# One kernel, two edges: where code transposes by DMA end, and what stands ahead of the tail columns on TensorE

## The chip, the core and the metric

One core of a Trainium2 chip runs the whole kernel. The metric is the time of the program in microseconds (us) on the device; one execution was also profiled.

## What is computed

The input is 8 sequences of 1,024 rows of 256 (64 tiles of 128 rows). A linear attention block with a layer norm is followed by a feed-forward block whose operands are quantised to FP4 in blocks of 16, and another layer norm:

```python
q = elu(x @ Wq + bq) + 1; k = elu(x @ Wk + bk) + 1; v = x @ Wv + bv     # 16 heads of 16
k = k / sqrt(sum(k * k, -1) + 1e-6)
out = (q @ (k^T @ v)) @ Wo + bo                                          # per head, no softmax
a = layernorm(x + out) * gamma + beta;  x1 = layernorm(x + a)

def fp4_linear(x, w):      # both sides: per block of 16 scale = max|.| / 6, values on the grid 0, 0.5, 1, 1.5, 2, 3, 4, 6
    return fp4_quant_dequant(x) @ fp4_quant_dequant(w).T
h = silu(fp4_linear(x1, w_gate)) * fp4_linear(x1, w_up)                  # 704 columns
result = layernorm(x1 + fp4_linear(h, w_down))
```

## The kernel before

**Stages.** While the keys, values and queries are projected (pairs of tiles p = 0 to 31), steps t of the second part already begin beside them: from p = 24 on the loop runs first(p) and step(p - 33). After that come steps 3 to 69 alone. Step t holds the pieces of many tiles at once: gate and up products of tile t, down product of tile t - 4, attention output of tile t + 9, layer norms of tiles t + 7, t + 5 and t - 6, quantisation of a "joint" tile that holds the 256 columns of x of tile n and the 704 columns of h of tile n - 4. There are five streams written out by hand, one for each engine, each in a fixed order; semaphores with counts connect them, and an engine that waits holds up all that stands behind in its stream.

**TensorE (PE), step(t), lines 641 to 657.** gate_up(t,0) and gate_up(t,1) are 512 columns each; gate_up(t,2) takes the remaining 192 columns of gate and up (the "tails"). turn(n) (L616) transposes the dequantised tile n in eight matmuls into PSUM. scales_turn(n) (L623) transposes the scales of a tile whose codes are transposed by DMA. attend(u) is L586, down(u) ends at L639. All products are split into high and low parts, L469 to L471.

**Two ways to turn a tile.** Odd tiles are dequantised on GpSimd (POOL; L1295, L1297) and turned on PE. Even tiles n from 12 to 66 are turned by DMA before they are dequantised: turn_codes (L428) transposes the 16-bit codes into wo_sb, the scales are transposed on PE, copied by ScalarE (ACT, L788), written to DRAM (L435, two of L439) and read back spread over all partitions (L445), and POOL multiplies the two (dequantise_turned, L1286). ACT makes the high parts of a turned tile (high_x L797, high_h L811 and L814) and, for tiles turned by DMA, copies it into PSUM (L801, L819); VectorE (DVE) makes the low parts, low_x (L1069) and low_h (L1076). For even tiles the waits of PE are on these.

**Quantisation of a tile.** DVE takes block maxima (amax_x L1031, amax_h L1037) and makes scales (L1050 to L1054); POOL divides (over_scales L1264 for h, L1267 for x); ACT converts (to_f16 L773, L775) and adds a rounding constant (add_half L782); DVE cuts the low bits (cut L1062). Then comes dequantise or turn_codes.

**ACT, step(t), lines 851 to 872:** high_h(t), silu(t,0) (L827), the three layer norm applications (L834, L839, L848), silu(t,1) (L829), high_x(t+1), scales_copy(t+3), to_f16(t+3), add_half(t+3). In the merged stretch first_keys(p) follows step: k_exps (L720), k_squares (L725). **DVE, step(t), lines 1106 to 1151:** residual (L1093), cut(t+2), amax_x, ln1_sum (L1099), statistics (L1121, L1124), low_h(t), gated(t,0) (L1085), statistics (L1131), three aggregates (L1104), gated(t,1) (L1087), amax_h(t+4), low_x(t+1), joint_scales(t+4). In the merged stretch first_keys(p) then makes the key features (L946) and values (L952); the queries' features are L936. **POOL:** roots(t) makes variance plus epsilon (L1249), the negative means (L1250), the power (L1252) and the product of the two (L1255); step(t) then dequantises, divides by scales, and applies gamma and beta (L1273, L1277). **SyncE (SP)** issues the DMAs in one queue: turn_codes(t+2), loads and stores of rows, repeat_scales(t+3), which waits on its own two or three small writes before L445.

**SHIFT.** For t below 6, turn(t+1), high_x(t+1) and low_x(t+1) stand before the tails, silu(t,1) and gated(t,1), and POOL dequantises tile t + 2 in step t; from t = 6 on they stand behind, and POOL dequantises tile t + 1.

Of the kernel before, what the change touches and what calls it, by code (L numbers as in the profile page):

```python
# [10 lines left out]
ALU = mybir.AluOpType  # L11
# [16 lines left out]
def after(eng, sem, count):  # L28

    if count > 0:  # L30
        eng.wait_ge(sem, count)


def build(nc, x, Wq, bq, Wk, bk, Wv, bv, Wo, bo, gamma, beta, w_gate, w_up, w_down, out):
# [24 lines left out]
    with ExitStack() as ctx:  # L59
# [116 lines left out]

        BY_DMA = 12
        codes = wo_sb[:, :, :].rearrange("p k d -> p (k d)").bitcast(U16).rearrange("p (c n) -> p c n", c=VC)  # L180
        s_each = resid[:, 0:4, :].rearrange("p t d -> p (t d)").rearrange("p (c n) -> p c n", c=VC)

# [92 lines left out]
        def there(t):  # L275
            return 0 <= t < T
# [4 lines left out]
        def joint(n):  # L281
            return there(n) or there(n - LAG)

        def by_dma(n):
            return joint(n) and n >= BY_DMA and (n - BY_DMA) % 2 == 0

        def earlier_by_dma(n):

            return max(0, (min(n, T + LAG) - BY_DMA + 1) // 2)

        def turned_on_pe(n):

# [33 lines left out]
        def rooted(t):  # L326
            return t + 8

        FIRST, LAST = -9, T + 5

        SHIFT = 6

        MERGE = NP - 8
        TAIL = 12
# [17 lines left out]
        def _(sp):  # L352
# [77 lines left out]
            def repeat_scales(n):  # L430
                i = earlier_by_dma(n)
                sp.wait_ge(sT_s, i + 1)
                after(sp, s_each_in, 16 * i)
                whole = (VC - 1) * GC
                sp.dma_start(s_turned[:, 0:VC - 1, :].rearrange("g c t -> c g t"), sT[0:whole, :]).then_inc(sT_out, 16)  # L435

                half = GC // 2
                for k in range(2):
                    sp.dma_start(s_turned[k * half:(k + 1) * half, VC - 1, :],  # L439
                                 sT[whole:whole + half, :]).then_inc(sT_out, 16)  # L440
                sp.wait_ge(sT_out, 3 * 16 * (i + 1))
                if i == 0:
                    sp.wait_ge(r3_s, 4)
                sp.wait_ge(deq_s, n - 1)
                sp.dma_start(s_each.rearrange("p c n -> p (c n)"),  # L445
                             s_turned.rearrange("g c t -> g (c t)").unsqueeze(1).broadcast_to(
                                 [GC, BLK, VC * P])).then_inc(s_each_in, 16)
# [16 lines left out]
        def _(pe):  # L464
# [176 lines left out]
            def step(t):  # L641
                if there(t):
                    pe.wait_ge(x_lo_s, t + 1)
                    gate_up(t, 0)
                    gate_up(t, 1)
                if joint(t + 1) and t < SHIFT:
                    turn(t + 1)
                if there(t):
                    gate_up(t, 2)
                if joint(t + 1) and t >= SHIFT and not by_dma(t + 1):  # L650
                    turn(t + 1)
                if by_dma(t + 3):
                    scales_turn(t + 3)
                if there(t + 9):
                    attend(t + 9)
                if there(t - LAG):
                    down(t - LAG)
# [16 lines left out]
        def _(act):  # L674
# [109 lines left out]
            def scales_copy(n):  # L784
                i = earlier_by_dma(n)
                act.wait_ge(sT_ps, i + 1)
                after(act, sT_out, 3 * 16 * i)
                nc.scalar.activation(sT[:, :], ps[0:VB, scales_bank(n), 0:P], ACT.Copy).then_inc(sT_s, 1)  # L788

            def high_x(n):  # L790
# [51 lines left out]
            def ln3_apply(u, t):  # L842
# [3 lines left out]
                if u % 2 == 0:  # L846
                    after(act, stored[u // 2 % 2], u // 4 * 16)
                nc.scalar.activation(ob[:, u // 2 % 2, u % 2, :], r3[:, u % 2, :], ACT.Identity, scale=rstd[:, t % 2, 2:3],  # L848
                                     bias=nmr[:, t % 2, 2:3]).then_inc(ob_s, 1)

            def step(t):
                if there(t - LAG):
                    high_h(t)
                if there(t):
                    silu(t, 0)
                if there(t + 7):
                    ln1_apply(t + 7, t)
                if there(t + 5):
                    ln2_apply(t + 5, t)
                if there(t - 6):  # L860
                    ln3_apply(t - 6, t)
                if there(t + 1) and t < SHIFT:
                    high_x(t + 1)
                if there(t):
                    silu(t, 1)
                if there(t + 1) and t >= SHIFT:
                    high_x(t + 1)
                if by_dma(t + 3):
                    scales_copy(t + 3)
                if joint(t + 3) and not pair(t + 33):  # L870
                    to_f16(t + 3)
                    add_half(t + 3)
# [14 lines left out]
        def _(dve):  # L887
# [177 lines left out]
            def low_x(n):  # L1065
                dve.wait_ge(x_hi_s, n + 1)
                if by_dma(n):
                    dve.wait_ge(x_ps, earlier_by_dma(n) + 1)
                nc.vector.tensor_tensor(vT_lo[:, n % 2, 0:XC, :], v_ps[:, 0:XC, :], f32(vT_hi[:, n % 2, 0:XC, :]),  # L1069
                                        ALU.subtract).then_inc(x_lo_s, 1)  # L1070
# [35 lines left out]
            def step(t):  # L1106
                n1, n2, n3 = there(t + 8), there(t + 6), there(t - 5)
                have = aggregated(t - 1)
                if n3:
                    residual(t - 5)  # L1110
                if joint(t + 2):
                    cut(t + 2)
                if there(t + 4):
                    amax_x(t + 4)
                if t == -1:
                    low_x(0)
                if n1:
                    ln1_sum(t + 8)
                if n3:
                    dve.wait_ge(r3_s, t - 4)  # L1120
                    nc.vector.bn_stats(st[:, 2, :], r3[:, (t - 5) % 2, :]).then_inc(st_s, 1)  # L1121
                if n1:
                    dve.wait_ge(y1_s, t + 9)
                    nc.vector.bn_stats(st[:, 0, :], y1[:, (t + 8) % 2, :]).then_inc(st_s, 1)  # L1124
                if there(t - LAG):
                    low_h(t)
                if there(t):
                    gated(t, 0)
                if n2:
                    dve.wait_ge(w1_s, t + 7)  # L1130
                    nc.vector.bn_stats(st[:, 1, :], w1[:, (t + 6) % 3, :]).then_inc(st_s, 1)  # L1131
                if n1 or n2 or n3:
                    after(dve, root_s, rooted(t - 1))
                if n3:
                    aggregate(2, t, have + 1)
                if n1:
                    aggregate(0, t, have + n3 + 1)
                if n2:
                    aggregate(1, t, have + n3 + n1 + 1)
                if there(t + 1) and 0 <= t < SHIFT:  # L1140
                    low_x(t + 1)
                if there(t):
                    gated(t, 1)
                    amax_h(t + 4)
                if there(t + 1) and t >= SHIFT:
                    low_x(t + 1)
                if joint(t + 4) and not pair(t + 33):
                    joint_scales(t + 4)
                for kind in range(2):
                    if t - 2 - kind in X_AGAIN:  # L1150
                        x_biases_again(X_AGAIN[t - 2 - kind], kind)
# [16 lines left out]
        def _(pool):  # L1168
# [71 lines left out]
            def roots(t):  # L1240
                if t < FIRST + 2:
                    return
                s = t % 2
                pool.wait_ge(agg_s, aggregated(t - 1))
                after(pool, z1_s, min(t + 6, T))
                after(pool, x1_s, min(t + 4, T))
                after(pool, ob_s, t - 7)
                after(pool, root_s, rooted(t - 1))
                nc.gpsimd.tensor_tensor(ve[:, :], mv[:, s, :, 1], eps_v[:, :], ALU.add).then_inc(ve_s, 1)  # L1249
                nc.gpsimd.tensor_tensor(nm[:, :], mv[:, s, :, 0], mone[:, :].broadcast_to([P, 3]), ALU.mult).then_inc(nm_s, 1)  # L1250
                pool.wait_ge(ve_s, rooted(t))
                nc.gpsimd.tensor_tensor(rstd[:, s, :], ve[:, :], mhalf[:, :].broadcast_to([P, 3]), ALU.pow).then_inc(pow_s, 1)  # L1252
                pool.wait_ge(pow_s, rooted(t))
                pool.wait_ge(nm_s, rooted(t))
                nc.gpsimd.tensor_tensor(nmr[:, s, :], nm[:, :], rstd[:, s, :], ALU.mult).then_inc(root_s, 1)  # L1255
# [44 lines left out]
            def step(t):  # L1300
                if t == FIRST + 2:
                    pool.wait_ge(late_in, 2 * 16)
                if by_dma(t + 1):
                    dequantise_turned(t + 1)
                elif joint(t + 1) and t > SHIFT:
                    dequantise(t + 1)
                if joint(t + 3):
                    over_scales(t + 3)
                if there(t + 7):
                    ln1_affine(t + 7)  # L1310
                if joint(t + 2) and t < SHIFT:
                    dequantise(t + 2)

            for p in range(-1, MERGE + TAIL):
# [32 lines left out]
```

## Time and profile before

| what | value |
|---|---|
| runs, us | 700.04, 700.3, 703.6 (median 700.3) |
| the profiled execution | 697.06 us, span 695.3 us |
| busy: PE, POOL, DVE, ACT | 96%, 88%, 82%, 77% |
| DMA | 79.3 MB, 58,726 packets |

The span runs from the first to the last instruction of the profiled execution; the rest of its time lies around it. Busy time is the time in which an engine's instructions run. In the profile's lines a name like banks<-wgu_hi,actT_lo is the tile written and the tiles read; L469 is a line of the kernel; an idle time in brackets names what ended it.

### The profile page before, as it was taken

The page shows a single profiled execution, that of the slowest core. Times are in us where ns is not written, and L with a number is a line of the kernel's source. Part 1 is how long each engine was busy: PE and PEld are TensorE (multiplying, and loading weights), DVE is VectorE, ACT ScalarE, POOL GpSimd, SP SyncE. Part 2 cuts the span into 40 slices and gives each one's busy share as a digit, 9 for nine tenths or more (in the row PEclk, how much of TensorE's full clock was granted, in tenths as well). Part 3 has the DMA queues.
Part 4 walks back from the last instruction along what each step waited for, and adds up shares of the span by engine and source line. Part 5 has one row for each costly group of instructions (what it writes and reads, how often), then busy time and mean ns, then how long its engine had stood idle before and what let it go on. Part 6 is the DMA issues. An engine that isn't in the chain of part 4 may idle for free.

```text
span 695.3 us, 14463 instructions
## 1 busy us (share of the span) xinstructions
PE 667.6 (96%) x4178; PEld 583.7 (84%) x4178; DVE 569.9 (82%) x1437; ACT 532.0 (77%) x1060; POOL 614.8 (88%) x919
## 2 busy tenths in 40 slices
PE   8999999999999899999999999999999999999964
PEld 6888888888877799889898998999989899987863
DVE  6678778776879888898898998989899898988752
ACT  5677777766677667788888888888888888888761
POOL 3988898988889999889999999999999999998663
PEclk9999999999999999999999999999999999999996
DMA  8543443344301111465655666557765576533640
GB/s 276 182 137 137 137 141 118 129 156 161 107 32 33 60 38 41 94 111 120 171 125 111 109 144 162 126 111 116 147 139 94 97 121 115 105 65 68 97 101 30
DMA packets 58726, 79.32 MB, mean 114 GB/s; under 512 B 32854, under 2 KB 37912, under 8 KB 58648
## 3 DMA queue, kind: packets, MB, share of 16 engines
q1 hardware_dynamic: 58228, 78.27, 47.3%
q8 instruction: 34, 0.56, 0.3%
q14 instruction: 44, 0.36, 0.1%
q10 hardware_dynamic: 420, 0.13, 0.1%
HBM read 44.90 MB, written 26.08 MB: 102 GB/s over the span
## 4 chain that ended last, share of the span: by engine, by line
PE 58%; POOL 19%; issue 10%; DVE 4%; DMA 4%; ACT 2%; SPq 1%; POOLq 0%; DVEq 0%; ACTq 0%
PE banks L469 15%; PE banks L470 14%; PE banks L471 14%; POOL arena L1264 5%; PE banks L586 4%; POOL arena L1297 3%; POOL arena L1286 3%; DMA resid<-scales_scratch 3%; PE banks L616 3%; POOL lnbuf L1273 3%; PE banks L507 2%; POOL arena L1267 2%; PE banks L480 2%; DVE actT_lo L1076 1%; PE banks L493 1%
## 5 line engine op out<-in xcount | busy, mean ns | idle before, releaser
L469 PE MATMUL banks<-wgu_hi,actT_lo 128*128 128x512 f32 (+1 forms) x384 | 145.6, 379 | 1.6 <-DVE resid L936 1.1
L470 PE MATMUL banks<-wgu_lo,actT_hi 128*128 128x512 f32 (+1 forms) x384 | 143.6, 374 | 0.0
L471 PE MATMUL banks<-wgu_hi,actT_hi 128*128 128x512 f32 (+1 forms) x384 | 143.3, 373 | 0.0
L469 PE MATMUL banks<-wd_hi,actT_lo 128*128 128x256 f32 x320 | 102.0, 319 | 4.0 <-DVE actT_lo L1076 4.0
L471 PE MATMUL banks<-wd_hi,actT_hi 128*128 128x256 f32 x320 | 91.7, 287 | 0.0
L470 PE MATMUL banks<-wd_lo,actT_hi 128*128 128x256 f32 x320 | 91.5, 286 | 0.0
L1264 POOL TENSOR_TENSOR arena<-arena 128x704 f32<-128x704 f32 x64 | 90.2, 1410 | 0.6 <-DVE arena L1054 0.6
L469 PEld LDWEIGHTS banks<-wgu_hi,actT_lo 128*128 128x128 f32 x384 | 72.3, 188 | 14.0 <-DVE actT_lo L1069 1.6
L471 PEld LDWEIGHTS banks<-wgu_hi,actT_hi 128*128 128x128 f32 x384 | 72.1, 188 | 10.6
L470 PEld LDWEIGHTS banks<-wgu_lo,actT_hi 128*128 128x128 f32 x384 | 72.4, 188 | 9.9
L1286 POOL TENSOR_TENSOR arena<-wo_sb,resid 128x1024 f32<-128x1024 f16 (+1 forms) x28 | 59.9, 2138 | 21.1 <-DMA wo_sb<-arena 20.9
L1252 POOL TENSOR_TENSOR rstd<-ve,mhalf 128x3 f32<-128x3 f32 x78 | 69.9, 897 | 0.0
L782 ACT ACTIVATE arena<-arena 128x1024 uint16<-128x1024 uint16 (+3 forms) x68 | 66.6, 980 | 2.2
L775 ACT ACTIVATE arena<-arena 128x960 f16<-128x960 bf16 (+2 forms) x68 | 64.6, 950 | 4.6 <-POOL arena L1267 3.8
L1222 POOL TENSOR_TENSOR xs<-arena 128x512 f32<-128x512 f32 x48 | 61.6, 1305 | 6.9 <-DMA arena<-in_L_attn_beta_dram 6.9
L469 PEld LDWEIGHTS banks<-wd_hi,actT_lo 128*128 128x128 f32 x320 | 61.9, 193 | 6.2 <-DVE actT_lo L1076 4.5
L1297 POOL TENSOR_TENSOR arena<-arena,s 128x960 f32<-128x960 f16 (+2 forms) x40 | 66.0, 1651 | 0.0
L586 PE MATMUL banks<-mo,resid 128*128 128x256 f32 x256 | 65.8, 380 | 0.0
L1093 DVE TENSOR_TENSOR arena<-banks,resid 128x256 f32<-128x256 f32 x64 | 26.8, 418 | 46.2 <-PE banks L639 46.2
L470 PEld LDWEIGHTS banks<-wd_lo,actT_hi 128*128 128x128 f32 x320 | 62.1, 194 | 1.3
L471 PEld LDWEIGHTS banks<-wd_hi,actT_hi 128*128 128x128 f32 x320 | 62.2, 194 | 0.0
L827 ACT ACTIVATE arena<-banks 128x512 f32<-128x512 f32 x64 | 37.7, 590 | 30.9 <-PE banks L471 30.8
(138 smaller groups left out, 2010.7 us busy)
## 6 DMA issues: line engine op xcount, KB each, us to landing
xs<-x_plus_scratch SPq DMA_DIRECT2D x32, 512.0 KB, 4.3
resid<-scales_scratch SPq DMA_DIRECT2D x28, 512.0 KB
x_plus_scratch<-xs SPq DMA_DIRECT2D x24, 512.0 KB, 2.9
arena<-in_L_attn_x_dram SPq DMA_DIRECT2D x32, 256.0 KB, 3.6
out_dram<-arena SPq DMA_DIRECT2D x32, 256.0 KB, 6.3
x_plus_scratch<-arena SPq DMA_DIRECT2D x4, 512.0 KB, 2.9
x_plus_scratch<-resid SPq DMA_DIRECT2D x4, 512.0 KB, 4.6
resid<-in_L_attn_x_dram SPq DMA_DIRECT2D x4, 256.0 KB, 6.0
```

The lines of the kernel that those rows point to most:

```text
L469: nc.tensor.matmul(dst, sl, mh, start=(k == 0), stop=False, skip_group_check=shared)
L470: nc.tensor.matmul(dst, sh, ml, start=False, stop=False, skip_group_check=shared)
L471: last = nc.tensor.matmul(dst, sh, mh, start=False, stop=(ended and k == n - 1), skip_group_check=shared)
L586: last = nc.tensor.matmul(ps[:, at_bank(u), 0:D], resid[:, u, m * P:(m + 1) * P], mo[:, u // TPB, m, :], start=(m == 0), stop=(m == KT - 1))
L775: nc.scalar.activation(vqb[n % 2][:, a // RW:b // RW, 0:RW].bitcast(F16), lines(halves(vy[:, n % 2, a:b])), ACT.Copy, scale=F16_ONE).then_ ...
L782: nc.scalar.activation(q, q, ACT.Copy, bias=ROUND_HALF).then_inc(half_s, 1)
L827: nc.scalar.activation(gact[:, 0:G0], ps[:, G_BANK, :], ACT.Silu).then_inc(g_act, 1)
L1222: nc.gpsimd.tensor_tensor(to[:, :, kind, :], xin[:, 2 * r:2 * r + 2, :], row[:, :].unsqueeze(1).broadcast_to([P, 2, D]), ALU.add).then_inc ...
L1252: nc.gpsimd.tensor_tensor(rstd[:, s, :], ve[:, :], mhalf[:, :].broadcast_to([P, 3]), ALU.pow).then_inc(pow_s, 1)
L1264: last = nc.gpsimd.tensor_tensor(blocks(vy[:, s, D:VW]), blocks(h[:, s, :]), each(inv[:, s, D // BLK:VB]), ALU.mult)
L1286: nc.gpsimd.tensor_tensor(v_turned(n)[:, a:VC, :], codes[:, a:VC, :].bitcast(F16), s_each[:, a:VC, :], ALU.mult).then_inc(deq_s, 1)
L1297: nc.gpsimd.tensor_tensor(blocks(va[:, (n + 1) % 2, a:b]), blocks(vqc[n % 2].bitcast(F16)[:, a:b]), each(s14[:, n % 4, a // BLK:b // BLK]) ...
```

## The change

- DMA_END = 56: only the even tiles 12 to 54 have their codes turned by DMA; tiles 56 to 66 are dequantised on POOL and turned on PE.
- UNSHIFT = 56: for t above 56 the order of the steps below SHIFT is used again (turn, high_x and low_x ahead of the tails, POOL a step ahead), and high_h and low_h of tiles above 57 are made a step earlier.
- In a step with by_dma(t + 3), scales_turn(t+3) and attend(t+9) stand before the tails, and ACT copies the scales before silu(t,1).
- The two writes of the last four scale rows become one with a broadcast source.
- The negative means are made by ACT (root_means) behind silu(t,1) of the step before, not by POOL in roots.

```diff
-        BY_DMA = 12
+        BY_DMA, DMA_END = 12, 56
...
         def by_dma(n):
-            return joint(n) and n >= BY_DMA and (n - BY_DMA) % 2 == 0
+            return BY_DMA <= n < DMA_END and (n - BY_DMA) % 2 == 0
...
-        SHIFT = 6
+        SHIFT, UNSHIFT = 6, 56
+
+        def late(t):
+            return SHIFT <= t <= UNSHIFT
+
+        def h_with_x(n):
+            return n > UNSHIFT + 1
...
-                for k in range(2):
-                    sp.dma_start(s_turned[k * half:(k + 1) * half, VC - 1, :],
-                                 sT[whole:whole + half, :]).then_inc(sT_out, 16)
-                sp.wait_ge(sT_out, 3 * 16 * (i + 1))
+                sp.dma_start(s_turned[:, VC - 1, :].rearrange("(k g) t -> g k t", k=2),
+                             sT[whole:VB, :].unsqueeze(1).broadcast_to([half, 2, P])).then_inc(sT_out, 16)
+                sp.wait_ge(sT_out, 2 * 16 * (i + 1))
...
-                if joint(t + 1) and t < SHIFT:
-                    turn(t + 1)
-                if there(t):
-                    gate_up(t, 2)
-                if joint(t + 1) and t >= SHIFT and not by_dma(t + 1):
+                if joint(t + 1) and not late(t):
                     turn(t + 1)
                 if by_dma(t + 3):
                     scales_turn(t + 3)
-                if there(t + 9):
+                    attend(t + 9)
+                if there(t):
+                    gate_up(t, 2)
+                if joint(t + 1) and late(t) and not by_dma(t + 1):
+                    turn(t + 1)
+                if there(t + 9) and not by_dma(t + 3):
                     attend(t + 9)
...
+            def root_means(t):
+                act.wait_ge(agg_s, aggregated(t - 1))
+                after(act, root_s, rooted(t - 1))
+                nc.scalar.activation(nm[:, :], mv[:, t % 2, :, 0], ACT.Copy, scale=-1.0).then_inc(nm_s, 1)
...
-                if there(t - LAG):
+                if there(t - LAG) and not h_with_x(t):
                     high_h(t)
...
+                if by_dma(t + 3):
+                    scales_copy(t + 3)
-                if there(t + 1) and t < SHIFT:
+                if there(t + 1) and not late(t):
                     high_x(t + 1)
+                if there(t + 1 - LAG) and h_with_x(t + 1):
+                    high_h(t + 1)
                 if there(t):
                     silu(t, 1)
-                if there(t + 1) and t >= SHIFT:
+                if FIRST + 2 <= t + 1 <= LAST + 1:
+                    root_means(t + 1)
+                if there(t + 1) and late(t):
                     high_x(t + 1)
-                if by_dma(t + 3):
-                    scales_copy(t + 3)
...
-                if there(t + 1) and 0 <= t < SHIFT:
+                if there(t + 1) and t >= 0 and not late(t):
                     low_x(t + 1)
+                if there(t + 1 - LAG) and h_with_x(t + 1):
+                    low_h(t + 1)
...
-                nc.gpsimd.tensor_tensor(nm[:, :], mv[:, s, :, 0], mone[:, :].broadcast_to([P, 3]), ALU.mult).then_inc(nm_s, 1)
...
-                elif joint(t + 1) and t > SHIFT:
+                elif late(t) and t > SHIFT:
                     dequantise(t + 1)
...
-                if joint(t + 2) and t < SHIFT:
+                if joint(t + 2) and not SHIFT <= t < UNSHIFT:
                     dequantise(t + 2)
```

## Rows read from the trace of the kernel before

**Rows 1.** The page's first part: busy time, share of the span and instructions of each engine.
```profile
PE 667.6 (96%) x4178; PEld 583.7 (84%) x4178; DVE 569.9 (82%) x1437; ACT 532.0 (77%) x1060; POOL 614.8 (88%) x919
```

**Rows 2.** The page's chain of waits: shares of the span by engine.
```profile
PE 58%; POOL 19%; issue 10%; DVE 4%; DMA 4%; ACT 2%; SPq 1%; POOLq 0%; DVEq 0%; ACTq 0%
```

**Rows 3.** Windows: length, busy us (instructions) of each engine, clock, DMA share, GB/s.
```profile
243.80:604.66 360.86, 359.77 (x2185) 326.99 (x2183) 324.23 (x901) 303.65 (x585) 340.55 (x474) 1.00 0.56 114
604.66:660.23 55.57, 52.38 (x319) 46.26 (x317) 46.31 (x110) 43.67 (x88) 45.95 (x64) 1.00 0.46 79
660.23:695.30 35.07, 19.84 (x118) 18.08 (x116) 14.43 (x32) 14.23 (x28) 18.72 (x36) 0.80 0.29 66
```

**Rows 4.** Waits of PE, 243.8 to 604.6 us: total, times, longest.
```profile
PE banks L616 <- DVE actT_lo L1076: 1.3, 3, 0.6
```

**Rows 5.** Timeline, step 41 and the start of step 42: start us, us, instruction.
```profile
503.89 0.40 PE L469 MATMUL banks<-wgu_hi,actT_lo 128*128 128x512 f32 x1
...
507.70 0.27 PE L623 MATMUL banks<-ident,s 128*60 128x128 f32 x1
507.81 1.03 PE L586 MATMUL banks<-mo,resid 128*128 128x256 f32 x4
508.49 0.47 PE L469 MATMUL banks<-wd_hi,actT_lo 128*128 128x256 f32 x1
...
509.48 0.41 DVE L1069 TENSOR_TENSOR actT_lo<-banks,actT_hi 128x256 fp32r<-128x256 f32 x1
...
510.70 0.40 PE L469 MATMUL banks<-wgu_hi,actT_lo 128*128 128x512 f32 x1
```

**Rows 6.** Timeline, end of step 57 (618.14 to 624.17) and start of step 58.
```profile
623.70 0.41 DVE L1069 TENSOR_TENSOR actT_lo<-banks,actT_hi 128x256 fp32r<-128x256 f32 x1
...
624.17 0.50 PE L469 MATMUL banks<-wgu_hi,actT_lo 128*128 128x512 f32 x1
```

**Rows 7.** Timeline, steps 41 and 42 (from 510.70): ACT, DVE, POOL and PE.
```profile
504.81 2.16 POOL L1286 TENSOR_TENSOR arena<-wo_sb,resid 128x1024 f32<-128x1024 f16 x1
...
510.13 1.06 ACT L782 ACTIVATE arena<-arena 128x1024 uint16<-128x1024 uint16 x1
510.70 1.01 POOL L1252 TENSOR_TENSOR rstd<-ve,mhalf 128x3 f32<-128x3 f32 x1
511.24 0.42 DVE L1062 TENSOR_SCALAR arena<-arena 128x1024 uint16<-128x1024 uint16 x1
512.18 1.79 POOL L1297 TENSOR_TENSOR arena<-arena,s 128x960 f32<-128x960 f16 x1
512.91 0.96 DVE L1076 TENSOR_TENSOR actT_lo<-banks,actT_hi 128x768 fp32r<-128x768 f32 x1
514.52 1.04 PE L616 MATMUL banks<-ident,arena 128*128 128x128 f32 x8
```

**Rows 8.** Timeline, step 58: DVE and POOL.
```profile
625.66 1.79 POOL L1297 TENSOR_TENSOR arena<-arena,s 128x960 f32<-128x960 f16 x1
626.37 1.37 DVE L1062 TENSOR_SCALAR arena<-arena 128x1024 uint16<-128x1024 uint16 x1 [1.28 <-ACT arena L782]
```

**Rows 9.** SP's timeline in step 42, and the landing of all transposes L428.
```profile
512.34 1.27 SPq L428 DMA_TRANSPOSE wo_sb<-arena  x1
...
DMA to landing us min/median/max: 5.5/6.7/7.2
```

**Rows 10.** Timeline of the merged stretch, p = 30: ACT and DVE.
```profile
192.73 0.67 ACT L720 ACTIVATE arena<-banks,mone 128x512 f32<-128x512 f32 x1
...
193.99 0.30 DVE L1104 BATCH_NORM_AGGREGATE mv<-st 128x2 f32<-128x6 f32 x2
194.21 0.67 DVE L946 SCALAR_TENSOR_TENSOR arena<-arena,banks 128x512 f32<-128x512 f32 x1
```

**Rows 11.** Waits from 660.2 us on (total, times, longest), and the last residual (timeline).
```profile
PE banks L616 <- DVE actT_lo L1076: 5.4, 2, 3.4
...
689.43 0.42 DVE L1093 TENSOR_TENSOR arena<-banks,resid 128x256 f32<-128x256 f32 x1 [2.90 <-PE banks L639]
```

More of the change, by code:

```diff
@@ L284, in by_dma @@
         def by_dma(n):
-            return joint(n) and n >= BY_DMA and (n - BY_DMA) % 2 == 0
+            return BY_DMA <= n < DMA_END and (n - BY_DMA) % 2 == 0
         def earlier_by_dma(n):
-            return max(0, (min(n, T + LAG) - BY_DMA + 1) // 2)
+            return max(0, (min(n, DMA_END) - BY_DMA + 1) // 2)
         def turned_on_pe(n):
@@ L786, in scales_copy @@
                 act.wait_ge(sT_ps, i + 1)
-                after(act, sT_out, 3 * 16 * i)
+                after(act, sT_out, 2 * 16 * i)
                 nc.scalar.activation(sT[:, :], ps[0:VB, scales_bank(n), 0:P], ACT.Copy).then_inc(sT_s, 1)
@@ L1124, in step @@
                     nc.vector.bn_stats(st[:, 0, :], y1[:, (t + 8) % 2, :]).then_inc(st_s, 1)
-                if there(t - LAG):
+                if there(t - LAG) and not h_with_x(t):
                     low_h(t)
@@ L1144, in step @@
                     amax_h(t + 4)
-                if there(t + 1) and t >= SHIFT:
+                if there(t + 1) and late(t):
                     low_x(t + 1)
```

## The prediction, made before the changed kernel ran

> **What bounds the kernel now.** I read the shares first: TensorE (PE) is busy for 96% of the span, GpSimd (POOL) for 88% [rows 1]. The chain of waits seems to contradict that, since it gives POOL 19% [rows 2]; so I cut the span into windows. Between 243.8 and 604.66 us, about fifty steps, PE is busy 359.8 of 360.9 us [rows 3]. The largest entry among its waits there is 1.3 us in three pieces, for L1076 [rows 4]. In this stretch PE's own work is the time, POOL only follows closely, and nothing that makes POOL or a DMA quicker can shorten it. The change can gain where PE waits: 3.2 us of the eight steps from 604.66, and above all the last 35.07 us, where PE is busy 19.84 us [rows 3]. It can lose where PE waits for nothing now.
>
> The profiled execution took 697.06 us (span 695.3); the median of the runs is 700.3, 3.2 above it. The sum is made on 697.06, and 3.2 is added at the end. Less than 0.5% (3.5 us) cannot be told from no change.
>
> **Odd steps: scales and attend ahead of the tails.** In the odd steps t = 9 to 51 the transposition of the scales and attend(t+9) now precede gate_up(t,2). Step 41 runs from 503.89 to 510.70, 6.81 us. The scales take 0.11 us (507.70 to 507.81). Attend takes 0.68 to the start of the first down product, and that product is 0.19 longer than the 0.28 of its followers, so 0.87 [rows 5]. PE's work stays the same, but the tails end 0.98 us later. Behind them hang silu(t,1), gated(t,1), amax_h and low_x(t+1), in this order, and the next gate_up waits for low_x. That ends now at 509.89, 6.00 after the step's start [rows 5]; it will end at 6.98. How PE takes this over is seen in step 57, which has no attend behind its tails: gate_up starts at 624.17, 0.06 after low_x's end at 624.11, and its first product takes 0.50 in place of 0.40 [rows 6]. So the next step starts at 7.04 in place of 6.81 and loses another 0.10: **0.33 us**. Step 9 has a turn behind its tails as cover; 21 steps x 0.33 = **+6.9 us**. The bounds are 0.2 (if the queue behind the tails catches up 0.1) and 0.4.
>
> **Even steps: the cut comes late.** ACT's to_f16 and add_half stand behind silu(t,1) in the same queue, and move 0.98 later too; the scales' copy of 60x128 leaves that place and the mean of 128x3 enters it, which I count as even. L782 ended at 511.19, 0.49 after the start of step 42 [rows 7]. In a step longer by 0.23 to 0.33 it will end about 1.05 after it, so DVE's cut of a DMA tile starts at 1.1 in place of 0.54. What does that cost? In step 42 the cut ends at 511.66, low_h (L1076) at 513.87, and the turn that waits for it starts at 514.52 [rows 7]: with 0.14 from low_h to the turn the cover is 0.5, so a cut may end 1.46 after the step's start; each us beyond that stops PE for a us. A cut of 0.42 started at 1.1 ends at 1.52, a stop of under **0.1 us**. That is one end.
>
> The other end is POOL. The cut of step 42 took 0.42 beside the small L1252 [rows 7]. The same operation took 1.37 in step 58, where it began 0.71 into L1297 and ended 0.29 behind that operation's end [rows 8]. I counted the cuts of DMA tiles: all six that met a long POOL operation took 1.29 to 1.72, the other 22 took 0.43. So where L1297 stands when the cut comes ready decides. L1297 follows L1286 by 7.2 us (the chain of POOL's operations from 504.81 to 512.18, less the mean's 0.15); L1286 follows L428 by its landing, median 6.7 us, and 0.2; and L428 follows the cut, since the scales' DMA no longer stands in front of it on SP (L428 was issued 0.68 behind the cut's end [rows 7, 9]). Two steps take 14.7 + s us, s being the stop, and s = end of cut - 1.46. L1297 thus starts at (cut end + 6.9 + 7.2) - (14.7 + s), about 0.85 into the even step whatever s is: ahead of the cut at 1.1. It then holds the cut until 0.85 + 1.79 + 0.29 = 2.9, a stop of **1.5 us**. With the fastest landing, 5.5 us [rows 9], L1297 starts 1.2 earlier and the stop is 0.3. The scales' transfer will be issued some 2 us sooner, so the codes share the queue with less of it; I take a landing of 6.1, half way between the fastest and the median: a stop of **0.85**. 21 x 0.85 = 17.9, less 1.1 that three early steps already lose to a late cut: **+16.8 us**, between +1 and +30.
>
> The page "SBUF — State Buffer" of the Trainium skill (Who interferes with whom) says that a VectorE operation in a two-port mode and a GpSimd operation exclude each other, and that the later one waits for the whole of the other. Rows 8 agree; rows 7 do not, for there the cut ran unhindered inside an operation of 1.01 us. By the rule without exception every cut would be held, and the sum would lie at its upper end.
>
> **The mean on ACT, in the merged stretch.** L1250 leaves POOL, where PE never waits for it: 0 in the steady state, and if its cover went, 0.15 us a step at most. On ACT it waits for DVE's aggregate (L1104). While keys are still projected, k_exps (L720) is queued behind it. Today L720 runs at 192.73, beside DVE's work, and L946 starts at 194.21, as the aggregate ends at 194.29 [rows 10]. Now L720 (0.67) and the mean come between them: up to 0.97 an iteration, and L946 leads over L725, the query maps and L936 back to the next aggregate, so it adds up. PE's slack in the first iterations takes a part. Of nine iterations I count 5 whole ones: **+5 us** (0 if another chain sets the iteration, 8 if all count).
>
> **The tail.** Tiles 56 to 66 go back to PE's transposes, which the odd tiles show to be there in steps of 7.58 with attend, so 6.7 without. Eight steps at 6.72 make 53.8 against 55.57 [rows 3]: **-1.8**. In the last stretch PE waits 5.4 us for low_h before its turns alone [rows 11]. With dequantise, turn, high_h and low_h of a tile a step ahead such waits go. What stays is one chain: tails of 63 (4.7 with turn(64) before them), silu to scales 2.8, L1264 1.4, to_f16 and add_half 1.6, cut 0.5, dequantise 2.3, turn 0.8, high_h and low_h 2.9, down 2.4, and the 5.87 from the last residual at 689.43 to the end [rows 11]: 25.2 against 35.07, **-9.9**. Half-clock products (the down at 0.5 of the clock takes 1.3 longer) make it 8.5 to 11.7.
>
> **Sum:** 697.1 + 6.9 + 16.8 + 5 - 1.8 - 9.9 = 714.1; with 3.2 for the median, **717 us**.
>
> **Rivals.**
> - *The cut gets in first.* If it starts before L1297, it ends at 1.52, and the even steps cost 2 in place of 17.9: 698.3, in the runs 701.5, no change to be told. For it: 0.25 us decides. Against it: the start of L1297 comes back to 0.85 by itself.
> - *Full collision.* The landing stays at its median: 1.5 a step, 731 us.
> - *Faster.* The decisive place is the queue behind the tails: if silu, gated and low_x take up the 0.98 (they would have to finish 0.3 sooner), the odd steps cost nothing, the cut comes in its old place, and with the merged stretch covered only the tail is left: 697.1 - 11.7 + 3.2 = 689. Against it: step 57 shows PE waiting in just this order with nothing moved.
> - *The tail does not speed up,* because one of its waits takes another's place: +10, 727.
>
> **How the numbers follow.** The forecast (a partial collision) 0.43, full collision 0.13, tail without gain 0.07; the cut first 0.20, which spreads around no change; faster 0.17. From these: faster 0.20, same 0.16, slower 0.64. The forecast's own range is 706 to 728. The range of 8 in 10 goes from 696, below the cut-first case with a cheap merged stretch, to 731, the full collision.
>
> **What would show it.** Right: odd steps of 7.1 in place of 6.81 with PE waiting for L1069; even steps over 8 with PE waiting for L1076, and cuts of 128x1024 of 1.3 us or more beside L1297; L946 later than the aggregate by L720; the last tile's tails within 26 us of the end. Wrong: odd steps still at 6.81, cuts at 0.43, or PE busy over 99% between steps 13 and 54.

## The result, and the profile after

The changed kernel takes 720.33 us (median of six runs, 719.67 to 724.19), the kernel before 703.48 over the six runs taken beside them: 1.0251 times as long, with a 95% interval of 1.0207 to 1.0296. Slower was forecast, with 717 us and a range of 696 to 731. The profiled executions lie further apart than the medians (spans 718.9 and 695.3), because the one of before is among its fastest; the comparison by steps below is made on these spans.

First the page of the changed kernel, busy time and the chain of waits, as [rows 1, 2].

```profile
PE 681.0 (95%) x4216; PEld 587.0 (82%) x4216; DVE 590.2 (82%) x1437; ACT 530.1 (74%) x1116; POOL 606.6 (84%) x847
...
PE 61%; DVE 15%; ACT 10%; issue 9%; POOL 2%; DMA 1%; DVEq 0%; SPq 0%; POOLq 0%; ACTq 0%
```

DVE and ACT now hold a quarter of the chain, where POOL had a fifth. Windows show where, as [rows 3]: steps 11 to 52, steps 55 to 62, and the rest.

```profile
293.62:625.05 331.43, 312.82 (x1829) 274.41 (x1828) 296.33 (x764) 261.43 (x547) 288.73 (x358) 1.00 0.46 113
639.34:693.20 53.86, 53.86 (x346) 49.34 (x345) 43.92 (x107) 39.10 (x80) 43.22 (x59) 1.00 0.06 21
693.20:718.90 25.70, 17.41 (x129) 16.09 (x127) 14.68 (x36) 13.39 (x29) 16.03 (x29) 0.98 0.11 41
```

In the middle PE is idle for 18.6 us, where it was idle for hardly any. The steps 11 to 52 take 28.0 us more than before; some 10 of these stand in PE's busy time, nearly all in gate products (+5.7) and transposes (+3.6): behind a stop the first gate product takes 0.50 in place of 0.40, and the next one starts 0.34 behind it in place of 0.24. The second window has no idle time left, and the last is 9.4 us shorter. By steps, in us of the two profiled executions:

| part | before | after | difference | forecast |
|---|---|---|---|---|
| start to step 0 | 207.4 | 212.7 | +5.2 | +5 |
| steps 0 to 10 | 79.5 | 81.0 | +1.5 | 0 |
| odd steps 11 to 51 | 143.0 | 148.2 | +5.1 | +6.9 |
| even steps 12 to 52 | 160.4 | 183.3 | +22.9 | +16.8 |
| steps 53 to 62 | 70.0 | 68.2 | -1.8 | -1.8 |
| step 63 to the end | 35.1 | 25.7 | -9.4 | -9.9 |

An odd step, 41, from 530.58 to 537.57 (timeline), as [rows 5]:

```profile
533.33 0.27 PE L630 MATMUL banks<-ident,s 128*60 128x128 f32 x1
533.44 1.03 PE L593 MATMUL banks<-mo,resid 128*128 128x256 f32 x4
...
537.10 0.42 DVE L1086 TENSOR_TENSOR actT_lo<-banks,actT_hi 128x256 fp32r<-128x256 f32 x1
...
537.57 0.50 PE L476 MATMUL banks<-wgu_hi,actT_lo 128*128 128x512 f32 x1
```

low_x (now L1086) ends 6.94 after the step's start, where 6.98 was forecast; the next gate_up follows 0.05 later, and the step takes 6.99 in place of 6.81. The even step after it, as [rows 7]:

```profile
537.65 1.06 ACT L790 ACTIVATE arena<-arena 128x1024 uint16<-128x1024 uint16 x1
538.54 1.40 POOL L1282 TENSOR_TENSOR arena<-arena 128x704 f32<-128x704 f32 x1
538.74 1.48 DVE L1079 TENSOR_SCALAR arena<-arena 128x1024 uint16<-128x1024 uint16 x1 [0.27 <-ACT arena L790]
...
541.47 0.93 DVE L1093 TENSOR_TENSOR actT_lo<-banks,actT_hi 128x768 fp32r<-128x768 f32 x1
...
542.54 1.06 PE L623 MATMUL banks<-ident,arena 128*128 128x128 f32 x8 [0.89 <-DVE actT_lo L1093]
```

The cut (L1079) starts 1.17 after the step's start, as forecast (1.1), and takes 1.48 in place of 0.42. The POOL operation beside it is not L1297's successor L1315, which the prediction named, but the next one, L1282 (over_scales): POOL stands further ahead than was reckoned. So it is for 18 of the 22 cuts of DMA tiles; the four in the steps 22, 28, 34 and 40 meet the end of L1315 and take 0.74 or 0.75. The step takes 8.77; with an end of the cut at 2.65, the prediction's relation (end less 1.46) gives a stop of 1.19, and that is the difference to 7.58. The waits over the steps 11 to 53 say the same, of PE and of its weight loads, as [rows 4]:

```profile
PE banks L623 <- DVE actT_lo L1093: 17.7, 21, 1.3
...
PEld banks L476 <- DVE actT_lo L1086: 5.0, 21, 0.2
```

### The profile page after: what moved, and what is told of

It reads as the page before. It is cut to its first block, busy times and chain, and to the rows that moved or that the text cites. A ratio compares the mean times of both kernels' runs of the same rounds, so it can differ in the third digit from the quotient of the medians.

```text
span 718.9 us, 14494 instructions
## 1 busy us (share of the span) xinstructions
PE 681.0 (95%) x4216; PEld 587.0 (82%) x4216; DVE 590.2 (82%) x1437; ACT 530.1 (74%) x1116; POOL 606.6 (84%) x847
## 4 chain that ended last, share of the span: by engine, by line
PE 61%; DVE 15%; ACT 10%; issue 9%; POOL 2%; DMA 1%; DVEq 0%; SPq 0%; POOLq 0%; ACTq 0%
PE banks L476 15%; PE banks L478 14%; PE banks L477 14%; PE banks L593 6%; PE banks L623 5%; DVE actT_lo L1093 4%; ACT arena L790 3%; ACT arena L783 3%; PE banks L514 2%; PE banks L487 2%; DVE arena L1048 2%; DVE lnbuf L1116 2%; DVE arena L1079 1%; DVE resid L985 1%; PE banks L500 1%
## 5 line engine op out<-in xcount | busy, mean ns | idle before, releaser
L476 PE MATMUL banks<-wgu_hi,actT_lo 128*128 128x512 f32 (+1 forms) x384 | 152.6, 397 | 2.2 <-DVE resid L953 1.4
L1282 POOL TENSOR_TENSOR arena<-arena 128x704 f32<-128x704 f32 x64 | 93.5, 1462 | 12.8 <-DVE arena L1071 12.8
L476 PE MATMUL banks<-wd_hi,actT_lo 128*128 128x256 f32 x320 | 96.3, 301 | 0.1
L1315 POOL TENSOR_TENSOR arena<-arena,s 128x960 f32<-128x960 f16 (+2 forms) x46 | 75.8, 1648 | 0.0
L1270 POOL TENSOR_TENSOR rstd<-ve,mhalf 128x3 f32<-128x3 f32 x78 | 67.0, 859 | 6.1
L1093 DVE TENSOR_TENSOR actT_lo<-banks,actT_hi 128x768 fp32r<-128x768 f32 x64 | 60.2, 940 | 9.7 <-ACT actT_hi L822 9.7
L623 PE MATMUL banks<-ident,arena 128*128 128x128 f32 x336 | 45.0, 275 | 22.8 <-DVE actT_lo L1093 21.5
L623 PEld LDWEIGHTS banks<-ident,arena 128*128 128x128 f32 x336 | 37.4, 141 | 32.5 <-issue 29.3
```

The source lines that it names most:

```text
L476: nc.tensor.matmul(dst, sl, mh, start=(k == 0), stop=False, skip_group_check=shared)
L623: last = nc.tensor.transpose(ps[:, T_BANK + c // 4, (c % 4) * P:(c % 4 + 1) * P], va[:, (n + 1) % 2, c * P:(c + 1) * P], ident[:, :])
L1093: nc.vector.tensor_tensor(vT_lo[:, n % 2, XC:VC, :], v_ps[:, XC:VC, :], f32(vT_hi[:, n % 2, XC:VC, :]), ALU.subtract).then_inc(h_lo_s, 1)
L1282: last = nc.gpsimd.tensor_tensor(blocks(vy[:, s, D:VW]), blocks(h[:, s, :]), each(inv[:, s, D // BLK:VB]), ALU.mult)
L1315: nc.gpsimd.tensor_tensor(blocks(va[:, (n + 1) % 2, a:b]), blocks(vqc[n % 2].bitcast(F16)[:, a:b]), each(s14[:, n % 4, a // BLK:b // BLK]) ...
```

## The experiments

The theory: attend ahead of the tails makes ACT's and DVE's work behind the tails late; in the odd steps this costs by low_x, in the even steps by a cut that meets a long POOL operation. The mean on ACT costs in the merged stretch (the steps that run beside the projections), and the tail gains.

**Attend back behind the tails**

```diff
                 if by_dma(t + 3):
                     scales_turn(t + 3)
-                    attend(t + 9)
                 if there(t):
                     gate_up(t, 2)
...
-                if there(t + 9) and not by_dma(t + 3):
+                if there(t + 9):
                     attend(t + 9)
```

> The changed kernel with one thing undone: attend(t+9) stands behind the tails again, scales_turn(t+3) alone stays ahead of them. Theory (the tails' delay by attend makes ACT late, and with it the cut): the tails move by 0.11 us only, odd steps return to 6.81 and even steps to 7.6 or 7.7, and nearly all of the 28.0 us that steps 12 to 52 gained go: 692 to 696 us against 720.3. Rival (the scales and codes that land earlier put POOL ahead, and POOL meets the cut whether ACT is late or not): even steps stay above 8.2 and the time above 708.

Measured: 702.51 us, 1.0014 times before (0.9977 to 1.0051). Of the loss in the middle two thirds went: steps 11 to 52 take 312.8 in place of 331.4, the odd steps are back at 6.8 but for three. But nine even steps still take 8.3 to 8.8, so the rival is right for a part: there is a loss that does not come from attend. The remaining 9.4 us over the kernel before are taken up below.

**The cut goes first**

```diff
+                if by_dma(t + 2):
+                    pool.wait_ge(round_s, t + 3)
                 if joint(t + 3):
                     over_scales(t + 3)
```

> The changed kernel with one wait more: in the even steps POOL's division by scales (over_scales) starts only when DVE has cut the tile t + 2. PE's, ACT's and DVE's orders stay. Theory (the shared port: the cut of 128x1024 is held by over_scales): the cuts take 0.43 us in place of 1.3 to 1.5, even steps come down from 8.75 to 7.7 to 7.9, odd ones stay at 7.0: about 20 us less, 699 to 702. Rival (the cut is late and long because ACT is late; POOL has no part in it): the even steps stay at 8.5 or more, and the time at 715 to 721.

Measured: 705.03 us, 15.3 less than the changed kernel, with the same order of PE, ACT and DVE. The timeline of step 42 (from 527.30):

```profile
528.48 0.43 DVE L1079 TENSOR_SCALAR arena<-arena 128x1024 uint16<-128x1024 uint16 x1 [0.27 <-ACT arena L790]
...
528.99 1.40 POOL L1282 TENSOR_TENSOR arena<-arena 128x704 f32<-128x704 f32 x1 [0.68 <-DVE arena L1079]
```

The cut starts at the same place and takes 0.43, and the step takes 7.77. What held it was POOL's operation; the late start alone, with a first product of 0.50 in place of 0.40, costs 0.19. The odd steps stay at 6.99 to 7.02, with four at 7.39. Eight even steps (20, 22, 26 and so on to 40) still take 8.2 to 8.3; in that part another DVE operation is held, x_biases_again (L985: 0.98 to 2.18 us, where it took 0.63 in seven of its eight calls before), see below, and in four of them the cut again (0.75, beside POOL's L1315). These twelve steps take some 5 us more than as many plain ones, enough for the distance to 699 to 702; no run tries it.

**low_x ahead of the maxima** (on top of the run before)

```diff
                     gated(t, 1)
+                if there(t + 1) and by_dma(t + 3):
+                    low_x(t + 1)
+                if there(t):
                     amax_h(t + 4)
-                if there(t + 1) and late(t):
+                if there(t + 1) and late(t) and not by_dma(t + 3):
                     low_x(t + 1)
```

> The run e2 (cut first) with one exchange on DVE: in the odd steps with scales to turn, low_x(t+1) stands before the block maxima of h, not behind them. Theory (the odd steps' 0.18 us is PE's wait for low_x, queued behind the maxima): odd steps return from 6.99 to 6.81, 21 x 0.18 = 3.8 us less than e2: 700 to 702 us. Rival (the odd steps are longer because scales and attend stand before the tails, whatever follows): no change from e2's 705.

Measured: 707.41 us, 2.4 more than the run before it, where 3.8 less was expected. The two profiled executions are 3.5 apart: 2.6 of that lies ahead of step 1, where both have the same code and the clock differs (told at the end). The odd steps are at 6.79 to 6.82 but for three at 7.19, so their 0.18 was the wait for low_x behind the maxima, as in the theory. But the plain even steps go from 7.77 to 8.04, and the sum of steps 11 to 52 is 317.1 against 316.2: DVE's chain is not shorter, only in another order. The timeline of DVE around the start of step 42 (530.27) shows where the time is given back:

```profile
529.55 0.42 DVE L1086 TENSOR_TENSOR actT_lo<-banks,actT_hi 128x256 fp32r<-128x256 f32 x1 [0.39 <-ACT banks L809]
529.89 0.88 DVE L1054 TENSOR_REDUCE arena<-arena 128x44 f32<-128x704 f32 x1
...
531.05 0.53 DVE L1071 RECIPROCAL arena<-arena 128x60 f32<-128x60 f32 x1
531.50 0.36 DVE L1110 TENSOR_TENSOR arena<-banks,resid 128x256 f32<-128x256 f32 x1
531.77 0.41 DVE L1079 TENSOR_SCALAR arena<-arena 128x1024 uint16<-128x1024 uint16 x1
```

The maxima and scales now run into the even step, and the cut starts at 1.50 in place of 1.18.

**The tail alone, on the kernel before**

```diff
-        BY_DMA = 12
+        BY_DMA, DMA_END = 12, 56
-        SHIFT = 6
+        SHIFT, UNSHIFT = 6, 56
```

with late(t), h_with_x(n) and what they steer; nothing of the scales' place, attend or the means.

> The kernel before with the tail's part alone: codes by DMA only up to tile 54, the early order from step 57, high_h and low_h a step earlier. Theory: steps 10 to 53 as before, the stretch from step 55 on shorter by 11 us: 690 to 693 us against 700 to 703. Rival (the tail is short only because the earlier steps were slow and left work done ahead): less than 6 us gained.

Measured: 689.07 us, 0.9828 times before (0.9776 to 0.9879). The gain is that of the changed kernel: the last windows,

```profile
609.24:663.11 53.87, 53.87 (x346) 49.36 (x345) 43.92 (x107) 38.41 (x72) 45.54 (x69) 1.00 0.06 20
663.11:688.92 25.81, 17.39 (x129) 16.07 (x127) 14.69 (x36) 12.34 (x22) 16.82 (x36) 0.98 0.11 42
```

are those of after to 0.1 us. So the one part of the change that gains does so alone.

**The means: late, and in other places of ACT's queue**

```diff
-                if FIRST + 2 <= t + 1 <= LAST + 1:
+                if 1 <= t + 1 <= LAST + 1:
                     root_means(t + 1)
```

with L1250 on POOL for the roots up to step 0.

> The changed kernel with the negative means left on POOL up to the roots of step 0, on ACT from the roots of step 1 on. Theory (the mean waits for the aggregate, and k_exps stands behind it on ACT): the start of step 0 returns from 212.7 to 207 us, all else as in the changed kernel: about 6.8 us less, 713 to 715. Rival (the merged stretch is slower for another reason, since its DMAs and PE's order there are unchanged): under 2 us gained.

Measured: 715.74 us, 4.6 less, where 6.8 was expected; in the profile step 1 starts at 215.55 in place of 221.32, 5.8 earlier. What the mean holds up stands in the changed kernel's timeline (ACT and DVE, last keys), as [rows 10]:

```profile
205.52 0.30 DVE L1121 BATCH_NORM_AGGREGATE mv<-st 128x2 f32<-128x6 f32 x2
205.85 0.21 ACT L862 ACTIVATE nm<-mv 128x3 f32<-128x3 f32 x1 [2.00 <-DVE mv L1121]
205.96 0.67 ACT L728 ACTIVATE arena<-banks,mone 128x512 f32<-128x512 f32 x1
206.66 0.69 DVE L963 SCALAR_TENSOR_TENSOR arena<-arena,banks 128x512 f32<-128x512 f32 x1 [0.85 <-ACT arena L728]
```

ACT is idle for 2.00 us until the aggregate is there, then makes the mean and k_exps (L728), and DVE's key features (L963) wait 0.85. Two runs keep the mean on ACT but move it. In the first it stands behind k_exps:

```diff
                 if pair(p):
                     k_exps(p)
+                if pair(p) and FIRST + 2 <= p - 32 <= LAST + 1:
+                    root_means(p - 32)
...
-                if FIRST + 2 <= t + 1 <= LAST + 1:
+                if FIRST + 2 <= t + 1 <= LAST + 1 and not pair(t + 33):
                     root_means(t + 1)
```

> The changed kernel with the negative means on ACT throughout, but in the merged stretch behind k_exps in ACT's queue, not ahead of it. Theory (only the order in the queue costs, not the mean's own 0.2 us): as e4, step 0 starts 4 to 6 us earlier, 714 to 716. Rival (a mean on ACT costs in this stretch wherever it stands, since the roots on POOL wait for it): 718 or more.

Measured: 717.3 us, between the two. One mean, that of root 0, is made after the last keys and kept its place, ahead of the last query maps. In the second run it moves behind those too:

> The run e7 with the one mean that still stands early (root 0, made in the iteration after the last keys) moved behind the last query maps in ACT's queue. Theory (that mean waits 2.1 us for DVE's aggregate at 211.04 us and holds the last query maps back): gate_up(0,1) starts at 211 to 212 us in place of 214.1, the whole at 713 to 715 against e7's 717.3. Rival (the mean on ACT costs where the roots on POOL wait for it, wherever it stands): gate_up(0,1) at 213 us or later, 716 or more.

Measured: 714.99 us. PE's waits before gate_up(0,1), first without and then with this last move:

```profile
214.08 0.80 PE L476 MATMUL banks<-wgu_hi,actT_lo 128*128 128x512 f32 x1 [2.70 <-DVE resid L955]
```

```profile
211.93 0.50 PE L476 MATMUL banks<-wgu_hi,actT_lo 128*128 128x512 f32 x1 [1.09 <-DVE resid L957]
```

In the changed kernel that product starts at 217.00, with the late means (e4) at 211.24. So the mean costs by its place in the queue; its own 0.2 us do not show. This last move also settles step 0: without it the product stands 4.36 behind the step's start, with it 2.77, as in the kernel before (2.76).

**What the early scales cost without attend.** The run with attend behind the tails, with all means back on POOL; the early scales and their single write stay:

> The run e1 (attend behind the tails again) with all negative means back on POOL; only the early scales and their single small write are left of the middle part. Theory (codes that land early are enough to put POOL ahead into the cut): the merged stretch gives back 5 to 6 us, steps 12 to 52 keep most of the 9 us that e1 has over the kernel before: 696 to 698. Rival (the 0.2 us that POOL saves by the means puts it ahead): those 9 us go as well: 688 to 690.

Measured: 702.3 us, so neither: the merged stretch gave its time back (step 1 at 216.45), but steps 11 to 52 rose to 317.7, 13.0 above the tail-only run. Of these, 11.4 us lie in the steps 20 to 22, 26 to 28, 32 to 34 and 38 to 40, and it is no cut that begins it there. The timeline at the end of step 25 (which ends at 401.85) and of step 26 (which ends at 411.38):

```profile
401.39 1.79 POOL L1308 TENSOR_TENSOR arena<-arena,s 128x960 f32<-128x960 f16 x1
...
401.74 1.99 DVE L977 TENSOR_TENSOR resid<-resid 128x512 f32<-128x512 f32 x1
...
403.99 1.28 DVE L1071 TENSOR_SCALAR arena<-arena 128x1024 uint16<-128x1024 uint16 x1
...
410.08 2.17 POOL L1297 TENSOR_TENSOR arena<-wo_sb,resid 128x1024 f32<-128x1024 f16 x1
...
410.68 2.12 DVE L977 TENSOR_TENSOR resid<-resid 128x512 f32<-128x512 f32 x1
...
412.21 1.84 POOL L1275 TENSOR_TENSOR arena<-arena 128x704 f32<-128x704 f32 x1
```

L977 is x_biases_again, an addition of two tiles in SBUF. It took 0.63 us (median) in the kernel before and 2.05 here (1.80 to 2.14 in all eight calls). POOL's operations have moved ahead into it: its dequantise of an odd tile (L1308) in the odd steps 19, 25, 31 and 37, its multiplication of a DMA tile (L1297) in the even steps behind them. The first of the two makes the cut late (L1071), and the even step takes 9.42 to 9.53 (11.35 in step 38, where the clock fell besides). And POOL's next operation takes 1.84 in place of 1.40, so the two hold each other up. The next run lets POOL make these additions, the one after it also holds POOL's dequantise until the cut is done.

> The run e6 (early scales and one small write, attend and means as before, the tail's part) with one more thing moved: the eight additions x_biases_again (128x512, both inputs in SBUF) are made by POOL at the end of the same steps, not by DVE. In e6 the steps 20, 26, 32 and 38, where DVE's addition runs beside POOL's dequantise_turned, take 9.4 to 11.35 us. Theory (in e6 it is this second kind of meeting that costs, about 11 of its 13 us over the tail-only kernel): these steps return to 7.6, 690 to 693 us. Rival (the early scales cost by DVE's cut meeting POOL, and POOL with more work meets it more often): 697 or more.

> The run e9 with POOL's dequantise of the even steps held until DVE's cut of tile t + 2 is done, so that neither kind of meeting is left. Theory (the early scales cost nothing of themselves, only through what POOL's earlier operations hold up): all middle steps at 6.8 and 7.6, 686 to 688 us, as e8, which has the scales late. Rival (the scales ahead of the tails cost PE or ACT something in each step): 690 or more.

```diff
-                nc.vector.tensor_tensor(xs_again[:, :, kind, :], x_again,
+                nc.gpsimd.tensor_tensor(xs_again[:, :, kind, :], x_again,
...
                 elif late(t) and t > SHIFT:
+                    if by_dma(t + 2):
+                        pool.wait_ge(round_s, t + 3)
                     dequantise(t + 1)
```

Measured: 692.63 and 690.57 us; steps 11 to 52 take 308.9 and 307.5. Of the 13.0 us, 8.9 go with the additions and 1.4 with the cut. What is left in the last run is a third thing (waits of PE, steps 11 to 53):

```profile
PE banks L623 <- POOL arena L1306: 3.6, 7, 0.6
```

PE waits for POOL's dequantise, in seven even steps from 22 to 40, beside the additions that POOL now makes (1.30 us each); the steps after 40 are all at 6.8 and 7.6. By its time (690.57, where 690 or more stood for it) the rival has it; the steps up to 19 and after 40 show no cost of the early scales by themselves. That the additions are what makes POOL late was not tried by itself. A gain of the early scales is in none of the runs.

**The tail, and the cut first**, on the kernel before:

> The run e3 (the tail's part alone) with e2's wait on POOL (over_scales of the even steps behind the cut). Theory (the cuts that met a POOL operation in steps 10 and 12 cost 1.6 us, the rest of the middle runs without a stop): 686.5 to 688.5 against e3's 689. Rival (POOL, held once in two steps, falls behind with the tiles that it dequantises): 690 or more.

Measured: 685.72 us, 0.9767 times before (0.9737 to 0.9798), faster than both kernels. The windows of steps 11 to 52:

```profile
289.57:591.94 302.37, 302.37 (x1830) 274.67 (x1829) 274.91 (x764) 260.61 (x505) 290.45 (x398) 1.00 0.60 124
```

PE is busy for all of it, and the cuts of DMA tiles take 0.41 to 0.46. So the wait on POOL costs nothing in this stretch; it sees to it that no cut is held.

## Why the prediction was right, and where it was not

**The bound.** That PE's own work is the time of the middle, and earlier codes can't shorten it, held: POOL waited 8.4 us for codes in the steps 6 to 53 before and 0.7 after, and nothing was won; the last run above reaches that bound, with PE never idle, with the scales sent as late as before.

**Odd steps: right, size too high.** 0.33 a step was forecast, 0.18 came in the plain ones: low_x was late as worked out, but it ended 0.04 sooner than reckoned, and the longer first product (0.10) disappears in the stop of the even step behind it. Four of them (21, 27, 33 and 39) take 7.3, 0.47 more than before. There x_biases_again, begun in the step ahead, takes 2.06 to 2.08 us and ends inside the odd step, which the prediction did not have. This was not tried by itself in the changed kernel; in the run with low_x first one such call took 0.63, and the odd step behind it 6.82 in place of 7.19. In all +5.1 for +6.9.

**Even steps: right in kind, with the wrong operation, and too low.** The late cut (1.17 for 1.1), the meeting with POOL and the price by the cut's end held, and the run with the cut first shows the meeting by itself: 15.3 of the loss. The step that failed is the loop by which L1297 was placed: it let POOL wait for a transpose landing after 6.1 us. With a landing half way between two rows of before, that was a guess at the one term that decided. The landings are now

```profile
DMA to landing us min/median/max: 3.2/4.1/5.2
```

(the transposes of the changed kernel, by their line) against [rows 9], so short that POOL hardly waits for them (0.7 us). It waits for DVE's aggregates (23.2 us over the steps 6 to 53, 2.2 before), and the operation that meets the cut is over_scales. The stop was mis-sized for that: 1.2 in a plain step, not 0.85; the size itself, between no stop and 1.5, was near by luck. The sum was +22.9 for +16.8.

**The port.** That a VectorE operation in a two-port mode and a GpSimd operation exclude each other, which "SBUF — State Buffer" of the Trainium skill states (Who interferes with whom), was left with an exception by [rows 7]. With the order turned round the cut takes 0.43 again. The same section of the Trainium skill says that a VectorE operation with two inputs in SBUF contends with a GpSimd operation that reads SBUF; the additions with the early scales (2.05 for 0.63) agree, and I had not looked for such operations in DVE's stream.

**The mean: right in kind, a little low.** +5.2 to step 0 for +5. The 1.5 us of the steps 0 to 10 are the mean's too: gate_up(0,1) starts 4.35 behind the start of step 0 in place of 2.76, because it waits for query features that the last mean holds back, and moving that one mean ends it (above). In all 6.7, for 5 and bounds of 0 to 8.

**The tail: right,** -1.8 and -9.4 for -1.8 and -9.9, and alone as good as with the rest. The granted clock of the last stretch is 0.98, where it was 0.80 [rows 3], so a part of this gain may be the clock's; no run takes the two apart.

The total of the terms was 17.0 against 23.6 in the spans; the forecast of 717 against 720.33 is nearer than that by luck. It had 3.2 us added because the median of before lay above its profile; in the changed kernel the median (720.33) lies at its profile (720.68), so that these 3.2 made up for half of what the terms lacked. The rival with the cut first did not come by itself, but made by a wait it came near what was worked out for it: 705 against 701.5.

## What to carry to other kernels

Moving work ahead on the engine that is the bound costs nothing on that engine, and yet makes everything late that hangs on what it was moved past: list the other engines' queues behind that result, with their covers, before anything is moved. Where VectorE and GpSimd both work all the time, a wait that lets the short operation go first can be worth more than an earlier start. In a queue, put an operation that waits for another engine behind those that feed that engine.

## What the runs showed of the hardware that was not expected

The granted clock falls from 2.4 to 1.2 GHz for a short stretch in step 0 or step 4 of some profiles, and in step 38 of the run without means on ACT (after a wait of 1.91 us). What a fall costs depends on whether PE waits there anyway. The stretch of step 0 up to gate_up(0,1), and from there to step 1, in the changed kernel and then in the run with low_x first:

```profile
212.65:217.00 4.35, 2.93 (x6) 0.61 0.00 0
217.00:221.32 4.32, 4.32 (x23) 1.00 0.07 12
...
213.37:217.70 4.33, 1.67 (x6) 1.00 0.00 0
217.73:223.60 5.87, 5.87 (x22) 0.71 0.24 89
```

The changed kernel was granted 0.61 (a mixture of the two levels) in the first part, after PE had waited 2.40 us in the queries just ahead of it. The fall cost nothing: with 1.00 the other kernel's first part is as long, since both wait for DVE's query features, 1.42 and 2.68 us. There the fall came behind that wait, in the second part, where PE never waits, and cost 1.6. With the means behind the keys it was the same: after a wait of 2.70, the first product took 0.80 for 0.50. All five profiles with waits of 2.4 to 2.7 us around step 0 have a fall there; in the eight others the waits are 0.9 to 1.1, and there is none.

In step 4 PE waits 1.9 us in every one of these kernels, with the same code. Nine of the thirteen profiles kept 1.00 there and took 9.74 to 9.77; four took 11.35 to 11.37. Step 4 of the kernel before and of the tail alone:

```profile
230.24:240.00 9.76, 7.87 (x49) 1.00 0.05 13
...
232.03:243.38 11.35, 9.47 (x49) 0.85 0.14 48
```

Near the span's start, too, some profiles had 0.5 for a stretch: three kernels that have the code of before up to step 0 (the tail alone, with the cut first, and the early scales without means on ACT) had it and started step 0 at 209.0 to 209.4, where before and the runs with POOL's additions did not and started it at 207.4 to 207.8. The run with low_x first had it too, the one with the cut first did not. So a difference of 1.6 us, or even 2, between two profiles of these kernels need not come from the edit.
